# A state-space scan on VectorE and its read-out on GpSimd: the read-out waits one drive longer, and the FFN's inner scaling changes engine

## The chip, the cores and the metric

The kernel runs on one core of a Trainium2 chip. The metric is device time in microseconds of one execution; lower is better. Engines are named TensorE (PE), VectorE (DVE), ScalarE (ACT), GpSimd (POOL) and SyncE (SP, which issues all transfers here).

## The reference, cut to what matters

16 sequences of 256 tokens with 128 channels pass four layers, each with a layer norm in front and a residual addition behind: a linear attention with random features, an FFN whose activations and weights are rounded to FP4 in blocks of 16, a selective state-space mixer (Mamba-like), and the same FFN again.

```python
x = x + attention(layernorm(x))
x = x + ffn(layernorm(x))
x = x + mixer(layernorm(x))
x = x + ffn(layernorm(x))

# mixer, the part that matters here: 256 inner channels, 16 states n
dA = exp(dt[..., None] * A)                     # "decay"
dBu = (dt * u)[..., None] * Bm[:, :, None, :]   # "drive"
h = dA_t * h + dBu_t                            # "scan" over the tokens
y = einsum('lbdn,bln->bld', hs, Cm)             # "read" times C, and a sum over n

# ffn: fp4_quant_dequant of the input of each product
h = silu(fp4_linear(x, w_gate)) * fp4_linear(x, w_up)
return fp4_linear(h, w_down)
```

## The kernel before, in words

The sequences go in eight groups of two (`SEQS`), 512 tokens each. The kernel is a software pipeline of ten turns over these groups. In turn i the group i is `new` (attention), i - 1 is `mid` (attention's end, first FFN `ffn_a`, the mixer up to its drives) and i - 2 is `old` (the mixer's scan and read-out, second FFN `ffn_b`). The order of the work on each engine is written out by hand: every engine has a `body(turn)` with two loops over 16 slots k, and the engines meet by semaphores only (`Events`; `at(group, n)` is the count after n events of that group).

The first loop is called the scan loop here. Slot k handles state k of the old group, in five steps:

- ScalarE: `decay_in`, two exponentials per state (L691), two buffers.
- VectorE: `drive` (L1032), `dtu` times the row of B, both 128x1024 and both in SBUF, result in two PSUM banks.
- VectorE: `scan` (L1043), one `tensor_tensor_scan` over 1024 elements, `decay` from SBUF and the drive from PSUM, result `state` in SBUF, three buffers.
- GpSimd: `read_out` (L566), `state` times the row of C, both in SBUF, result `read`, three buffers.
- TensorE: `sum_states` (L1301), matmuls with the identity that add `read` into two PSUM banks, two slots later.

The rows of B and C (`bc_row`, 512 KB per state, four buffers) are loaded by SyncE; a load waits for the read four states earlier. There is a single PSUM buffer for the drive, so drive k + 1 waits for scan k and scan k + 1 for drive k + 1.

Beside this, each engine's `attention_rest(turn, k)` carries the other work of the slot: statistics of the norms in slots 0, 2 and 15 (`statistics` on VectorE, `deviation` on GpSimd, `normalise` on ScalarE), rounding of the FFN's input in slots 3 and 4, squares and Newton steps of the attention's norms in slots 6 to 10 (GpSimd's Newton steps in slot 9, VectorE's two multiplications L1109 in slot 10), and the FFN's hidden layer for two pairs of tiles: `hidden_start` in slots 7 and 11, `hidden_end` in 8 and 12 (VectorE), then `scale_hidden` in 8 and 12 (GpSimd, L551 and L556: subtract the rounding constant, multiply by the block scale), then `hidden_t` and `down` in 10 and 14 (TensorE) and `ffn_result` in 11 and 14 (VectorE, L1011).

The second loop, called the feature loop here, computes the attention's features, scores and context of the new group (`features` L1017 and L1023, `mask` L1053) and `mixer_rest`: the rest of the mixer for old and mid, and `ffn_b`. Its start needs TensorE's `project` of slot 1, which stands behind `sum_states` of states 14 and 15 in TensorE's order.

Before the change VectorE's slot reads scan k, drive k + 1, other work, and GpSimd's slot reads read k, other work. The last turn has only an old group, and in it the FFN of the group before (`ffn_b_aside`) runs beside the scans, with `scale_hidden` on GpSimd in slots 2 and 6.

Of the kernel before, what the change touches and what calls it, by code (L numbers as in the profile page):

```python
# [19 lines left out]
ALU = mybir.AluOpType  # L20
# [25 lines left out]
SLOTS = SEQS * PAIRS  # L46
# [52 lines left out]
def build(nc, x_in, w_qkv_t, b_qkv, w_out_t, b_out, omega_t, nodes, weights, ln_g, ln_b, in_wx_t,  # L99
# [17 lines left out]
    with ctx:  # L117
# [374 lines left out]
        def _(pool):  # L492
# [68 lines left out]
            def read_out(group, s):  # L561

                pool.wait_ge(state_done.sem, state_done.at(group, s + 1))

                pool.wait_ge(y_ps.sem, y_ps.at(group, max(s + 1 - STATE_BUFFERS, 0)))
                pool.tensor_tensor(  # L566
                    read[:, s % STATE_BUFFERS], state[:, s % STATE_BUFFERS],
                    bc_row[:, s % BC_BUFFERS, 1].unsqueeze(1).broadcast_to([P, DT, TOK]), ALU.mult).then_inc(
                        read_done.sem, 1)

            def attention_rest(turn, k):
# [5 lines left out]
                if turn.has_new and k == 3:  # L577
# [5 lines left out]
                    pool.tensor_tensor(  # L583
                        xab[:], xa[:], bout[:].unsqueeze(1).broadcast_to([P, TILES, C]), ALU.add
                    ).then_inc(residual.sem, 1)
                if turn.has_mid and k in (8, 12):
                    scale_hidden(ffn_a, mid, (k - 8) // 4)
                if turn.is_last and k in (2, 6):
                    scale_hidden(ffn_b_aside, late, (k - 2) // 4)
                if turn.has_new and k == 9:  # L590
# [56 lines left out]

            def body(turn):
                for k in range(SLOTS):
                    if turn.has_old:  # L650
                        read_out(turn.old, k)
                    attention_rest(turn, k)
                for k in range(SLOTS):
                    mixer_rest(turn, k)
                if turn.is_last:
                    scale_hidden(ffn_b, turn.old, 0)
                    scale_hidden(ffn_b_last, turn.old, 1)
# [238 lines left out]
        def _(dve):  # L896
# [107 lines left out]
            def hidden_end(f, group, pair):  # L1004
                round_end(f, group, f.quant_h, f.h[:].rearrange("p t n -> p (t n)"), 8 + 7 * pair
                          ).then_inc(f.h_lifted.sem, 1)

            def ffn_result(f, group, pair, x_src, dst):
                dve.wait_ge(f.down_ps.sem, f.down_ps.at(group, pair + 1))
                tiles = slice(2 * pair, 2 * pair + 2)  # L1010
                dve.tensor_tensor(  # L1011
                    dst[:, tiles], f.out, x_src[:, tiles], ALU.add).then_inc(f.result.sem, 1)
# [60 lines left out]
            def attention_rest(turn, k):  # L1073
# [26 lines left out]
                    hidden_start(ffn_a, mid, (k - 7) // 4)  # L1100
                if turn.has_mid and k in (8, 12):
                    hidden_end(ffn_a, mid, (k - 8) // 4)
                if turn.has_new and k == 10:
                    dve.wait_ge(rnorm_done.sem, rnorm_done.at(new, 1))
                    for b in range(SEQS):
                        rows = slice(CHUNKS * b, CHUNKS * (b + 1))
                        cols = slice(CHUNKS * 2 * HEADS * b, CHUNKS * 2 * HEADS * (b + 1))
                        v = qk[:, rows].rearrange("p t (h d) -> p (t h) d", d=HD)
                        dve.tensor_tensor(  # L1109
                            v, v, rnorm[:, cols].unsqueeze(2).broadcast_to(  # L1110
                                [P, CHUNKS * 2 * HEADS, HD]), ALU.mult).then_inc(zn_done.sem, 1)
# [74 lines left out]
            def body(turn):  # L1186
                for k in range(SLOTS):
                    if turn.has_old:
                        scan(turn.old, k)
                        if k + 1 < SLOTS:  # L1190
                            drive(turn.old, k + 1)
                    if turn.has_mid and k == 0:
                        attention_out(turn.mid, SEQS - 1)
                    attention_rest(turn, k)
                if turn.has_new:
                    features(turn.new, 0)
                for k in range(SLOTS):
# [428 lines left out]
```

## Time and profile before

| | |
|---|---|
| median of 3 runs | 1839.3 us (1839.26 to 1842.27) |
| the profiled execution | 1841.2 us, span of its instructions 1839.4 us |
| VectorE busy | 1398.6 us (76% of the span) |
| TensorE busy, matmuls | 1178.1 us (64%) |
| ScalarE busy | 730.8 us (40%) |
| GpSimd busy | 651.6 us (35%) |
| mean granted clock of TensorE | 0.780 of full speed |
| transfers | 74.74 MB, mean 41 GB/s |

All durations below are of the one profiled execution, in microseconds from the start of its span unless ns is written. Busy time is the time in which an engine executes an instruction; where an instruction is held up after it has started, the holding is inside its duration. The idle time of an engine is put down to what ended it.

### The profile page before, as it was taken

What the parts mean: (1) busy time and instruction counts of PE and PEld (TensorE: products, weight loads), DVE (VectorE), ACT (ScalarE), POOL (GpSimd) and SP (SyncE); (2) the same over time, 40 slices, a digit from 0 to 9 for tenths busy, and PEclk for the clock granted to TensorE, in tenths of its full rate; (3) what the DMA queues carried; (4) which work ended last, traced back from release to release, by engine and by line L of the source; (5) the groups of instructions that cost most, each with busy time, mean ns of one, the idle gap of its engine ahead of it and who ended that gap; (6) DMA issues with size and microseconds to landing.
All of it is one profiled execution on the core that took longest, in us unless ns stands there. A gap on an engine that the chain in (4) does not pass through costs nothing. (4 is left out here: it accounts for less than half of the span.)

```text
span 1839.4 us, 14293 instructions
## 1 busy us (share of the span) xinstructions
PE 1178.1 (64%) x4361; PEld 591.2 (32%) x4361; DVE 1398.6 (76%) x1535; ACT 730.8 (40%) x1293; POOL 651.6 (35%) x484
## 2 busy tenths in 40 slices
PE   4966864786557775587647866477745874444554
PEld 1433332343223432244323432233422442221212
DVE  1744699777996789866997779967898669965964
ACT  2534642554326533264324543255332642243211
POOL 2012244323353144422444233531345223452531
PEclk9967876897768976788778977689767887775765
DMA  2000122010210112001220102101110011202210
GB/s 55 1 6 1 48 75 68 0 48 29 75 46 1 48 58 68 23 1 53 75 68 1 48 29 74 46 1 48 52 68 24 0 54 69 69 0 80 77 33 6
DMA packets 31404, 74.74 MB, mean 41 GB/s; under 512 B 4505, under 2 KB 14562, under 8 KB 31330
## 3 DMA queue, kind: packets, MB, share of 16 engines
q1 hardware_dynamic: 31330, 73.83, 11.7%
q8 instruction: 37, 0.61, 0.1%
q14 instruction: 37, 0.30, 0.1%
HBM read 71.20 MB, written 2.62 MB: 40 GB/s over the span
## 5 line engine op out<-in xcount | busy, mean ns | idle before, releaser
L566 POOL TENSOR_TENSOR read<-state,bc_row 128x1024 f32<-128x1024 f32 x128 | 316.4, 2472 | 453.5 <-DVE state L1043 449.9
L1032 DVE TENSOR_TENSOR bank<-dtu,bc_row 128x1024 f32<-128x1024 f32 x128 | 382.9, 2992 | 34.1 <-POOL dtu L644 20.8
L1301 PE MATMUL bank<-read,ident 128*128 128x512 f32 x512 | 328.5, 783 | 100.7 <-POOL read L566 100.7
L1043 DVE TENSOR_TENSOR_SCAN state<-decay,bank 128x1024 f32<-128x1024 f32 x128 | 291.6, 2278 | 4.7 <-ACT decay L691 0.5
L691 ACT ACTIVATE decay<-dt,neg_a 128x510 f32<-128x510 f32 x256 | 169.3, 711 | 287.6 <-DVE state L1043 286.5
L1301 PEld LDWEIGHTS bank<-read,ident 128*128 128x128 f32 x512 | 120.7, 252 | 246.1 <-issue 123.5
L1053 DVE TENSOR_TENSOR s_sb<-bank,causal 128x512 f32<-128x512 f32 x128 | 87.9, 687 | 134.0 <-PE bank L1251 134.0
L1249 PE MATMUL bank<-feat 64*128 64x256 f32 x512 | 118.1, 487 | 95.2 <-ACT s_sb L702 95.1
L1238 PE MATMUL bank<-znt,omega 128*128 128x512 f32 x256 | 152.0, 678 | 40.2 <-ACT sqf L682 40.2
L679 ACT ACTIVATE expf<-bank,minus_s,root2s 128x512 f32<-128x512 f32 x128 | 99.8, 780 | 119.1 <-PE bank L1238 118.7
L1275 PE MATMUL bank<-s_sb,vext 128*32 128x256 f32 (+1 forms) x1024 | 131.9, 358 | 2.9 <-DVE att L1068 2.4
L702 ACT ACTIVATE s_sb<-bank 128x256 f32<-128x256 f32 x128 | 49.1, 384 | 205.1 <-DVE s_sb L1053 205.1
L1023 DVE SCALAR_TENSOR_TENSOR feat<-expf,scale_f,sqf 128x512 f32<-128x512 f32 x128 | 119.3, 932 | 5.5
L1017 DVE TENSOR_SCALAR expf<-expf 128x512 f32<-128x512 f32 x128 | 87.6, 685 | 37.7 <-ACT expf L679 37.7
L1326 PE MATMUL bank<-ident,a_ffn_h 128*128 128x128 f32 (+1 forms) x102 | 26.2, 430 | 129.6 <-POOL a_ffn_h L556 129.6
L1249 PEld LDWEIGHTS bank<-feat 64*128 64x128 f32 x512 | 51.9, 211 | 166.5 <-issue 151.3
L551 POOL TENSOR_TENSOR b_ffn_rounded<-b_ffn_rounded,b_ffn_magic 128x704 f32<-128x704 f32 x15 | 26.4, 1761 | 187.8 <-DVE b_ffn_rounded L970 187.8
L682 ACT ACTIVATE sqf<-bank 128x512 f32<-128x512 f32 x128 | 76.2, 595 | 0.0
L1238 PEld LDWEIGHTS bank<-znt,omega 128*128 128x128 f32 x256 | 45.2, 205 | 90.3 <-issue 85.6
L1275 PEld LDWEIGHTS bank<-s_sb,vext 128*32 128x32 f32 x1024 | 40.8, 114 | 102.2 <-issue 68.1
L1251 PEld LDWEIGHTS bank<-feat 64*128 64x128 f32 x512 | 68.8, 219 | 7.0
L1251 PE MATMUL bank<-feat 64*128 64x128 f32 x512 | 65.6, 303 | 0.0
(223 smaller groups left out, 1893.3 us busy)
## 6 DMA issues: line engine op xcount, KB each, us to landing
bc_row<-bc_rows SPq DMA_DIRECT2D x128, 512.0 KB, 3.6
xa<-x_dram SPq DMA_DIRECT2D x8, 256.0 KB, 2.7
out_dram<-x SPq DMA_DIRECT2D x8, 256.0 KB, 2.3
omega<-omega_t_dram SPq DMA_DIRECT2D x1, 512.0 KB
bc_rows<-xdbl SPq DMA_DIRECT2D x8, 64.0 KB
wqkv<-w_qkv_t_dram SPq DMA_DIRECT2D x1, 192.0 KB
state<-w_down_dram SPq DMA_DIRECT2D x1, 176.0 KB, 2.5
state<-w_gate_dram SPq DMA_DIRECT2D x1, 128.0 KB, 2.1
```

The costliest lines, as they stand in the source:

```text
L566: pool.tensor_tensor(read[:, s % STATE_BUFFERS], state[:, s % STATE_BUFFERS], bc_row[:, s % BC_BUFFERS, 1].unsqueeze(1).broadcast_to([P, D ...
L679: act.activation(expf[:, s % 2], bank[:, 0], ACT.Exp, bias=minus_s[:], scale=root2s[:]).then_inc(exp_done.sem, 1)
L691: last = act.activation(decay[:, s % 2, k, :, 1:], dt[:, k].rearrange("p (b t) -> p b t", b=SEQS)[:, :, 1:], ACT.Exp, scale=neg_a[:, k, s: ...
L1023: dve.scalar_tensor_tensor(feat[:, s % 2], expf[:, s % 2], scale_f[:], sqf[:, s % 2], ALU.mult, ALU.mult).then_inc(feat_done.sem, 1)
L1032: dve.tensor_tensor(bank[:, DRIVE_BANK:DRIVE_BANK + DT], dtu[:], bc_row[:, s % BC_BUFFERS, 0].unsqueeze(1).broadcast_to([P, DT, TOK]), ALU ...
L1043: dve.tensor_tensor_scan(state[:, s % STATE_BUFFERS].rearrange("p k t -> p (k t)"), decay[:, s % 2].rearrange("p k b t -> p (k b t)"), ban ...
L1053: dve.tensor_tensor(s_sb[:, s % S_BUFFERS].rearrange("p h (k t) -> p h k t", t=P)[:, :, 0:3:2], bank[:, 1:3, 0:SEQ + P].rearrange("p h (k ...
L1238: pe.matmul(bank[:, 0], omega[:, j], znt[:, b], start=True, stop=True).then_inc(proj_ps.sem, 1)
L1249: pe.matmul(bank[:, 1 + h, 0:SEQ], f[:, SEQ:SEQ + P], f[:, 0:SEQ], start=True, stop=True)
L1251: last = pe.matmul(bank[:, 1 + h, SEQ:SEQ + P], f[:, SEQ + P:], f[:, P:SEQ], start=True, stop=True)
L1275: last = pe.matmul(o, columns, scored, start=(k == 0 and below == 0), stop=(k == 1 and below == 1))
L1301: last = pe.matmul(bank[:, 6 + k], ident[:], read[:, s % STATE_BUFFERS, k], start=(s == 0), stop=(s == STATES - 1))
```

## The change

Three things are altered.

1. `read_out` on GpSimd has one more wait: the read of state s waits until drive s + 1 is done (for the last state there is no further drive, and the wait asks for what is long done).
2. VectorE's slot becomes scan k, other work, drive k + 1; GpSimd's slot becomes other work, read k.
3. `scale_hidden` of `ffn_a` leaves GpSimd; VectorE does the same two steps right behind `hidden_end` (`hidden_scaled`). `ffn_b` and `ffn_b_aside` keep theirs on GpSimd.

```diff
@@ -562,6 +562,8 @@  (GpSimd, read_out)
                 pool.wait_ge(state_done.sem, state_done.at(group, s + 1))
 
+                pool.wait_ge(drive_done.sem, drive_done.at(group, min(s + 2, STATES)))
+
                 pool.wait_ge(y_ps.sem, y_ps.at(group, max(s + 1 - STATE_BUFFERS, 0)))
@@ -583,8 +585,6 @@  (GpSimd, attention_rest)
-                if turn.has_mid and k in (8, 12):
-                    scale_hidden(ffn_a, mid, (k - 8) // 4)
                 if turn.is_last and k in (2, 6):
                     scale_hidden(ffn_b_aside, late, (k - 2) // 4)
@@ -647,9 +647,9 @@  (GpSimd, body)
                 for k in range(SLOTS):
+                    attention_rest(turn, k)
                     if turn.has_old:
                         read_out(turn.old, k)
-                    attention_rest(turn, k)
@@ -1005,6 +1005,19 @@  (VectorE)
+            def hidden_scaled(f, group, pair):
+                q = f.quant_h
+                dve.wait_ge(f.h_lifted.sem, f.h_lifted.at(group, pair + 1))
+                dve.tensor_tensor(q.rounded, q.rounded, q.magic, ALU.subtract).then_inc(
+                    f.h_rounded.sem, 1)
+                dve.wait_ge(f.h_rounded.sem, f.h_rounded.at(group, pair + 1))
+
+                dve.wait_ge(f.ht_ps.sem, f.ht_ps.at(group, pair))
+                dve.tensor_tensor(
+                    blocks(f.hq[:].rearrange("p t n -> p (t n)")),
+                    blocks(q.rounded), across(q.scale[:], q.blocks), ALU.mult).then_inc(
+                        f.hq_done.sem, 1)
@@ -1100,6 +1113,7 @@  (VectorE, attention_rest)
                 if turn.has_mid and k in (8, 12):
                     hidden_end(ffn_a, mid, (k - 8) // 4)
+                    hidden_scaled(ffn_a, mid, (k - 8) // 4)
@@ -1187,11 +1201,11 @@  (VectorE, body)
                 for k in range(SLOTS):
                     if turn.has_old:
                         scan(turn.old, k)
-                        if k + 1 < SLOTS:
-                            drive(turn.old, k + 1)
                     if turn.has_mid and k == 0:
                         attention_out(turn.mid, SEQS - 1)
                     attention_rest(turn, k)
+                    if turn.has_old and k + 1 < SLOTS:
+                        drive(turn.old, k + 1)
```

Two places show how the order moves. The first is VectorE around slots 7 to 9 of a middle turn. Before:

```order
L1032 TENSOR_TENSOR bank<-dtu,bc_row 128x1024
L990 SCALAR_TENSOR_TENSOR a_ffn_h<-a_ffn_h,bank 128x704
L995 TENSOR_TENSOR a_ffn_h<-a_ffn_h,bank 128x704
L947 TENSOR_REDUCE a_ffn_qh_scale<-a_ffn_h 128x44
L950 TENSOR_SCALAR a_ffn_qh_scale<-a_ffn_qh_scale 128x44
L953 RECIPROCAL a_ffn_qh_inv<-a_ffn_qh_scale 128x44
L955 TENSOR_TENSOR a_ffn_h<-a_ffn_h,a_ffn_qh_inv 128x704
L1043 SCALAR_TENSOR_TENSOR state<-decay,bank 128x1024
L1032 TENSOR_TENSOR bank<-dtu,bc_row 128x1024
L964 TENSOR_SCALAR a_ffn_magic<-a_ffn_h 128x704
L967 TENSOR_SCALAR a_ffn_magic<-a_ffn_magic 128x704
L970 TENSOR_TENSOR a_ffn_rounded<-a_ffn_h,a_ffn_magic 128x704
```

And of the change, where L1045 is the drive and L1056 the scan (the order names the scan's instruction SCALAR_TENSOR_TENSOR):

```order
L1045 TENSOR_TENSOR bank<-dtu,bc_row 128x1024
L1056 SCALAR_TENSOR_TENSOR state<-decay,bank 128x1024
L964 TENSOR_SCALAR a_ffn_magic<-a_ffn_h 128x704
L967 TENSOR_SCALAR a_ffn_magic<-a_ffn_magic 128x704
L970 TENSOR_TENSOR a_ffn_rounded<-a_ffn_h,a_ffn_magic 128x704
L1011 TENSOR_TENSOR a_ffn_rounded<-a_ffn_rounded,a_ffn_magic 128x704
L1016 TENSOR_TENSOR a_ffn_h<-a_ffn_rounded,a_ffn_qh_scale 128x704
L1045 TENSOR_TENSOR bank<-dtu,bc_row 128x1024
L1056 SCALAR_TENSOR_TENSOR state<-decay,bank 128x1024
```

The slot's other work now stands between scan and next drive, so that a scan follows each drive at once, and two 128x704 steps (L1011, L1016) have been added in slots 8 and 12.

The second place is GpSimd at the end of the scan loop, where the last reads and slot 15's deviation of `norm_b` stand. Before:

```order
L566 TENSOR_TENSOR read<-state,bc_row 128x1024 [waits b_y_in_psum,b_state] x3
L531 TENSOR_SCALAR b_ln_rstd<-b_ln_mv 128x4 [waits b_ln_var]
L533 TENSOR_SCALAR b_ln_rstd<-b_ln_mv 128x4
L535 TENSOR_SCALAR b_ln_shift<-b_ln_mv 128x4
L539 TENSOR_TENSOR b_ln_rstd<-b_ln_rstd,minus_half 128x8 [waits b_ln_eps]
L543 TENSOR_TENSOR b_ln_shift<-b_ln_shift,b_ln_rstd 128x4 [waits b_ln_rstd_ready]
```

And of the change:

```order
L568 TENSOR_TENSOR read<-state,bc_row 128x1024 [waits b_y_in_psum,b_drive,b_state] x6
L531 TENSOR_SCALAR b_ln_rstd<-b_ln_mv 128x4 [waits b_ln_var]
L533 TENSOR_SCALAR b_ln_rstd<-b_ln_mv 128x4
L535 TENSOR_SCALAR b_ln_shift<-b_ln_mv 128x4
L539 TENSOR_TENSOR b_ln_rstd<-b_ln_rstd,minus_half 128x8 [waits b_ln_eps]
L543 TENSOR_TENSOR b_ln_shift<-b_ln_shift,b_ln_rstd 128x4 [waits b_ln_rstd_ready]
L543 TENSOR_TENSOR b_ln_shift<-b_ln_shift,b_ln_rstd 128x4
L568 TENSOR_TENSOR read<-state,bc_row 128x1024 [waits b_y_in_psum,b_drive,b_state]
```

The read of state 15 has moved behind the deviation, and every read has the drive among its waits.

## Rows read from the trace of the kernel before

**Rows 1.** Windows of turn 5: stretch, length, busy times, granted clock, DMA share, GB/s.

```profile
870.40:984.80 114.40, 65.83 (x178) 32.77 (x172) 110.15 (x94) 36.66 (x65) 52.13 (x33) 0.73 0.18 60
984.80:1085.40 100.60, 78.27 (x371) 40.72 (x372) 65.24 (x99) 54.04 (x96) 29.19 (x26) 0.85 0.06 22
```

**Rows 2.** Costliest groups, whole span: busy us, mean ns of one, idle before.

```profile
L1032 DVE TENSOR_TENSOR bank<-dtu,bc_row 128x1024 f32<-128x1024 f32 x128 | 382.9, 2992 | 34.1 <-POOL dtu L644 20.8 <-DVE state L1043 0.9
L566 POOL TENSOR_TENSOR read<-state,bc_row 128x1024 f32<-128x1024 f32 x128 | 316.4, 2472 | 453.5 <-DVE state L1043 449.9 <-PE bank L1301 3.5
L1043 DVE TENSOR_TENSOR_SCAN state<-decay,bank 128x1024 f32<-128x1024 f32 x128 | 291.6, 2278 | 4.7 <-ACT decay L691 0.5
L1109 DVE TENSOR_TENSOR qk<-qk,rnorm 128x512 f32<-128x512 f32 x16 | 23.1, 1485 | 16.6 <-POOL rnorm L602 16.6
...
L955 DVE TENSOR_TENSOR a_ffn_h<-a_ffn_h,a_ffn_qh_inv 128x704 f32<-128x704 f32 x17 | 15.2, 892 | 0.6
```

**Rows 3.** Instructions that touch bc_row: least, median and most ns of one.

```profile
L1032 DVE TENSOR_TENSOR bank<-dtu,bc_row x128: 1223/3410/3424, 224.7 to 1772.5; 128x1024 f32<-128x1024 f32 x128
L566 POOL TENSOR_TENSOR read<-state,bc_row x128: 2340/2351/3334, 228.8 to 1778.4; 128x1024 f32<-128x1024 f32 x128
```

**Rows 4.** VectorE's timeline, two drives in turn 5: start, us, instruction.

```profile
912.11 3.42 DVE L1032 TENSOR_TENSOR bank<-dtu,bc_row 128x1024 f32<-128x1024 f32 x1
...
918.00 3.41 DVE L1032 TENSOR_TENSOR bank<-dtu,bc_row 128x1024 f32<-128x1024 f32 x1
```

**Rows 5.** Timeline of all engines in slots 8 and 9 of turn 5.

```profile
940.30 2.28 DVE L1043 TENSOR_TENSOR_SCAN state<-decay,bank 128x1024 f32<-128x1024 f32 x1
940.46 1.67 POOL L551 TENSOR_TENSOR a_ffn_rounded<-a_ffn_rounded,a_ffn_magic 128x704 f32<-128x704 f32 x1 [3.08 <-DVE a_ffn_rounded L970]
942.21 1.39 POOL L556 TENSOR_TENSOR a_ffn_h<-a_ffn_rounded,a_ffn_qh_scale 128x704 f32<-128x704 f32 x1
...
942.68 2.00 DVE L1032 TENSOR_TENSOR bank<-dtu,bc_row 128x1024 f32<-128x1024 f32 x1
...
947.16 1.23 DVE L1032 TENSOR_TENSOR bank<-dtu,bc_row 128x1024 f32<-128x1024 f32 x1
947.32 1.38 POOL L596 TENSOR_TENSOR newton_t<-newton_t,sumsq_qk 128x128 f32<-128x128 f32 x1
```

**Rows 6.** Timelines of GpSimd, ScalarE and VectorE, slots 2 and 3 of turn 5.

```profile
893.25 0.20 POOL L531 TENSOR_SCALAR a_ffn_ln_rstd<-a_ffn_ln_mv 128x4 f32<-128x4 f32 x1 [3.09 <-DVE a_ffn_ln_mv L940]
...
897.72 2.25 POOL L583 TENSOR_TENSOR xab<-xa,bout 128x512 f32<-128x512 f32 x1
...
895.12 1.65 ACT L667 ACTIVATE a_ffn_xq<-x,a_ffn_ln_shift,a_ffn_ln_rstd 128x128 f32<-128x128 f32 x4 [6.03 <-POOL a_ffn_ln_shift L543]
...
899.47 0.54 DVE L950 TENSOR_SCALAR a_ffn_qx_scale<-a_ffn_qx_scale 128x32 f32<-128x32 f32 x1
```

**Rows 7.** Timelines of GpSimd, TensorE and VectorE where the feature loop begins.

```profile
983.79 2.35 POOL L566 TENSOR_TENSOR read<-state,bc_row 128x1024 f32<-128x1024 f32 x1 [3.69 <-DVE state L1043]
...
989.33 0.36 POOL L543 TENSOR_TENSOR b_ln_shift<-b_ln_shift,b_ln_rstd 128x4 f32<-128x4 f32 x2
...
986.20 1.99 PE L1301 MATMUL bank<-read,ident 128*128 128x512 f32 x4 [1.21 <-POOL read L566]
988.02 1.02 PE L1238 MATMUL bank<-znt,omega 128*128 128x512 f32 x2
...
984.50 0.38 DVE L940 BATCH_NORM_AGGREGATE b_ln_mv<-b_ln_stats 128x2 f32<-128x6 f32 x4
...
989.89 0.43 DVE L1017 TENSOR_SCALAR expf<-expf 128x512 f32<-128x512 f32 x1 [2.68 <-ACT expf L679]
```

**Rows 8.** TensorE's timeline from the second pair's hidden values, turn 5.

```profile
974.27 1.54 PE L1326 MATMUL bank<-ident,a_ffn_h 128*128 128x128 f32 x6 [4.72 <-POOL a_ffn_h L556]
975.61 3.62 PE L1301 MATMUL bank<-read,ident 128*128 128x512 f32 x4
979.02 1.67 PE L1337 MATMUL bank<-wdown,a_ffn_ht 128*128 128x128 f32 x12
```

## The prediction

> **What bounds the kernel now.** I read the windows first, then the costliest groups, the spread of single instructions, and the timeline of one group. The program alternates two loops of 16 slots. In turn 5 the scan loop takes 114.4 us, with VectorE busy for 110.2 of them, so VectorE sets it; the feature loop takes 100.6 us with VectorE busy for 65.2 and no engine full, so chains across engines set it [rows 1]. Eight scan loops run, and seven feature loops lie between them. Most of the predicted gain therefore has to come from VectorE's busy time in the scan loop, and most of the loss from a later start of a feature loop.
>
> In the groups, the drive (L1032) costs 382.9 us in 128 instructions, the scan (L1043) 291.6, GpSimd's read (L566) 316.4 [rows 2]. The reader is to see that drive and scan handle equally many elements, yet the drive's mean is 2992 ns; its spread is 1223/3410/3424 ns (least, median, most), while the read's is 2340/2351/3334 [rows 3]. The two states differ by what GpSimd does: in a slot without other work the drive starts at 912.11 and takes 3.42, and the next starts 5.89 us later [rows 4]. The read is released by the same scan as the drive, so they start together, and 3.41 is the read's 2.35 plus most of a drive of 1.22. The reverse is there too: a drive starts at 947.16 and runs its 1.23, and a small GpSimd multiplication that starts 0.16 after it takes 1.38, ending 0.31 after the drive [rows 5]. The scan, by contrast, at 940.30 keeps its 2.28 while GpSimd works from 940.46 on through the scan; the drive behind it is caught and takes 2.00 [rows 5]. So reads block drives and do not touch scans.
>
> GpSimd's durations carry this argument. The Trainium skill (Perfetto Trace Analysis, GPSIMD spans) warns that they are unreliable and that start-to-start spacing is to be used. The spacing agrees here: a blocked drive is 3.41 - 1.22 = 2.19 longer, as measured on VectorE itself.
>
> **Edit 1: the read waits for the next drive.** The read of slot s then runs beside scan s+1. From the drive's end the read ends at 0.08 + 2.35 = 2.43; the scan ends at about 2.37, and the next drive, released by it, starts at 2.47. They miss each other by a hair. Every drive at 1.22: 382.9 - 128 x 1.22 = 226.7 us saved [rows 2, 3]. What is queued behind the wait is GpSimd's next work and TensorE's sum of that state; TensorE is 58% busy in the loop (65.8 of 114.4 [rows 1]) and reads three buffers deep, so in a steady slot nobody needs the sum. Where VectorE has other work after the scan, the read's last 0.15 us block its first instruction if that has two SBUF inputs: about 4 slots in 7 loops, **+4 us**.
>
> **Edit 2: other work between scan and drive; on GpSimd its share ahead of the read.** This costs nothing by itself, but GpSimd's order makes some reads late. Costs, from the trace:
> - Slot 0, six loops: after the statistics GpSimd's deviation takes 1.85 us, by its twin of slot 2 that begins at 893.25 and releases ScalarE at 895.12 [rows 6], but VectorE's drive goes first (1.22), so it ends 3.0 after the statistics, and the read 0 behind it at 5.4. Drive 2 is due at 3.7 and is held 1.7: **+10 us**.
> - Slots 2 and 3, seven loops: again the deviation ends at 3.0; ScalarE's normalising takes 1.65 [rows 6], so VectorE, there at 3.6, waits to 4.75, about 1.15. Then the read to 5.4 and the residual addition (2.25 in contention [rows 6], half that alone) hold the next small step: today that costs 0.35 (0.54 where 0.19 is usual), I take 1.4. Together 2.2 in six loops and 1.2 in the draining one: **+14 us**.
> - Slot 9: the Newton steps and the multiplications by them lose, over 8 turns, 16.6 idle and 23.1 - 16 x 0.69 = 12.1 blocked [rows 2], 3.6 a turn (0.69 lies on one line with 1.22 for 1024 elements and 0.89 for 704). The new order brings the Newton steps ahead of the read but keeps a read beside the multiplications. Between no gain and 3.6 I take half: **-11 us** in six loops.
> - Slot 15, the largest: read 15 was released by scan 15 at 983.79 and its sum ran at 986.20, then the projection at 988.02 [rows 7]. That projection releases the exponential for which VectorE waited 2.68 [rows 7]. Now the statistics, which end at 984.88, 1.15 after the scan, and the deviation, which took from the read's end at 986.14 to 989.69 [rows 7], stand ahead of read 15: 1.15 + 3.55, and some 0.3 more for the feature steps that block it, 5.0 later. Nothing covers this, since the feature loop starts from that projection: **+34 us** (six times 5.0, and once 4.1 where no feature steps block). Bounds: nothing, if the earlier deviation pays it back, and 6.
> - The last turn keeps its two pairs of hidden scaling on GpSimd, at slots 2 and 6, ahead of the read. The backlog holds one drive by 0.6 and the next by 2.25: **+6 us**.
>
> **Edit 3: the hidden layer on VectorE.** 28 multiplications and subtractions in seven scan loops, 128x704 with two SBUF inputs, 892 ns each by VectorE's step of the same shape [rows 2], 0.92 with the wait between: **+26 us**. GpSimd loses 1.67 + 1.39 a pair [rows 5], which gives nothing directly. In turn 1, bound by its chain, the shorter step gives perhaps **-2 us**. The second half's result is now closer: from the hidden values TensorE's chain is transposes at 974.27, a sum at 975.61 (3.4), down projection 1.67 [rows 8]. The sum waits for read 12, which ends 3.65 after the hidden values; 3.65 + 3.4 + 1.67 = 8.7 against VectorE's 7.3: a wait of 1.5 in seven loops, **+10 us** (bounds 0 and 3).
>
> **Sum.** -226.7 + 4 + 10 + 14 - 11 + 34 + 6 + 26 - 2 + 10 = -136 us. The profiled execution took 1841.2, which gives 1705; the median of the runs is 1839.3, 1.9 lower, so **1704 us**. Per middle turn the scan loop should fall from 114.4 to about 94.5 and the feature loop rise from 100.6 to about 105.5.
>
> **The clock, weighed.** The scan loop had a granted clock of 0.73 [rows 1]; the sum at 975.61 took 3.6 and the one at 986.20 took 1.99 [rows 7, 8], the two levels of 1.2 and 2.4 GHz. I keep the slow sum. The Trainium skill (TensorE: Matmul & The Clock Gate, the HAM clock gate) says that idling lowers the clock and activity restores it; a denser scan loop would by that run faster, which is the first rival.
>
> **Rivals.**
> 1. Denser TensorE work at 2.4 GHz. The same matmuls in 94 us instead of 114 leave shorter gaps. The second-half wait goes (-10), the sum and projection of slot 15 are seldom slow already; if the early deviation also pays back half of the slot 15 delay (-17) and slot 3's wait shrinks (-8), the time is 1704 - 35 = 1669. For it: 0.85 granted in the fuller feature loop [rows 1]. Against: nearly all this work is still released one read at a time. Chance 0.2.
> 2. Chains become the bound. With slots of 3.7 instead of 5.9 us, TensorE's backlog after the projections of slot 3 (at 1.2 GHz a sum of 3.5 fills a slot) can hold ScalarE's tanh and VectorE's slot 7; at 5 us for seven loops, 1740. Against: 65.8 us of TensorE fit into 94. Chance 0.15.
> 3. Slower: the scan pays. It reads its decay from SBUF as the drive reads its operands; if a read beside it blocked it, each of 120 scans would be 2.35 longer where the drive gains 2.19: +19 instead of -227 for the main term, with the other terms +91, so about 1950. It decides from the point where a scan lengthens by (227 - 91) / 120 = 1.1 us. The scan at 940.30 and the spread of all 128 (the group's mean is 2278 [rows 2]) speak against it. Chance 0.03.
> 4. The change does not do what it says: the new wait is already over when the read comes to it, so drives stay at 3.4. Only if GpSimd were always late; it idled 453.5 us before reads [rows 2]. Then about 1839 + 60 = 1900. Chance 0.01.
>
> **How the numbers follow.** The forecast has 0.61, its own range 1685 to 1725 from the bounds above. With rivals 1 and 2 taken in, the range is 1660 to 1745. A measurement here can tell 0.2%, 3.7 us, from no change; only rivals 3 and 4 are above that: faster 0.95, same 0.01, slower 0.04.
>
> **What would show it.** Right: the drive's median near 1.23, the scan's still 2.28, the read's releaser the drive, VectorE's new steps 0.9, read 15 some 5 us after the last scan, a scan loop near 94 and a feature loop near 105. Wrong: scans beyond 3 us; drives with a median over 2; VectorE idle in slots 7 or 11 for TensorE; a feature loop of 100 (then slot 15 cost nothing, and the time is near 1670).

## The result, and the profile after

| | before | after |
|---|---|---|
| median | 1839.52 us (4 runs) | 1705.95 us (4 runs) |
| lowest to highest | 1839.26 to 1842.27 | 1705.04 to 1709.21 |
| ratio | | 0.9274, 95% interval 0.9258 to 0.929 |
| profiled execution, its span | 1841.22, 1839.4 | 1706.21, 1704.1 |
| mean granted clock | 0.780 | 0.811 |
| VectorE busy | 1398.6 (76%) | 1206.6 (71%) |

The change saves 133.6 us; 136 were predicted. In the changed kernel the drive is L1045, the scan L1056, the read L568, the sum over states on TensorE L1315, the down projection L1351.

The costliest groups of the kernel after (busy us, mean ns of one, idle before it and what ended that):

```profile
L1315 PE MATMUL bank<-read,ident 128*128 128x512 f32 x512 | 344.2, 810 | 234.2 <-POOL read L568 234.0
L568 POOL TENSOR_TENSOR read<-state,bc_row 128x1024 f32<-128x1024 f32 x128 | 301.8, 2359 | 328.8 <-DVE bank L1045 249.4 <-issue 75.0 <-PE bank L1315 4.5
L1056 DVE TENSOR_TENSOR_SCAN state<-decay,bank 128x1024 f32<-128x1024 f32 x128 | 292.7, 2287 | 11.9 <-ACT decay L691 0.5
...
L1045 DVE TENSOR_TENSOR bank<-dtu,bc_row 128x1024 f32<-128x1024 f32 x128 | 168.8, 1319 | 25.4 <-POOL dtu L644 20.8 <-DVE state L1056 0.5
...
L1123 DVE TENSOR_TENSOR qk<-qk,rnorm 128x512 f32<-128x512 f32 x16 | 17.0, 1101 | 3.9 <-POOL rnorm L602 3.9
...
L1011 DVE TENSOR_TENSOR a_ffn_rounded<-a_ffn_rounded,a_ffn_magic 128x704 f32<-128x704 f32 x16 | 14.3, 892 | 0.5
L1016 DVE TENSOR_TENSOR a_ffn_h<-a_ffn_rounded,a_ffn_qh_scale 128x704 f32<-128x704 f32 x16 | 14.3, 892 | 0.5
```

Against [rows 2]: the drives fell from 382.9 to 168.8 us, 214.1 less; the scans stayed (2278 ns each before, 2287 now); the read's releaser is the drive; L1011 and L1016 are new on VectorE, 892 ns each.

Instructions that touch bc_row, after (least/median/most ns of one), to be read against [rows 3]:

```profile
L1045 DVE TENSOR_TENSOR bank<-dtu,bc_row x128: 1206/1226/3133, 223.6 to 1645.0; 128x1024 f32<-128x1024 f32 x128
L568 POOL TENSOR_TENSOR read<-state,bc_row x128: 2337/2342/3332, 232.5 to 1648.6; 128x1024 f32<-128x1024 f32 x128
```

The median drive went from 3410 to 1226 ns while the read kept its length: two instructions that had met no longer meet.

Windows of the kernel after: the scan loop and the feature loop of turn 5, and the last turn's scan loop (start:end and length, busy times, granted clock, DMA share, GB/s):

```profile
824.00:917.00 93.00, 64.06 (x177) 30.62 (x174) 87.56 (x99) 36.18 (x65) 43.65 (x28) 0.81 0.22 74
917.00:1023.70 106.70, 80.64 (x373) 41.41 (x373) 63.97 (x97) 53.99 (x96) 30.14 (x26) 0.84 0.06 21
1567.50:1648.50 81.00, 47.19 (x100) 19.78 (x100) 71.19 (x52) 22.73 (x36) 44.72 (x19) 0.71 0.24 81
```

The scan loop of turn 5 fell from 114.4 to 93.0 us, and its feature loop rose from 100.6 to 106.7 [rows 1]. VectorE is now 94% busy in the scan loop (87.56 of 93.00); before it was 96%.

What VectorE waited for (us in total, times, longest), first before, then after:

```profile
DVE x L1011 <- PE bank L1337: 46.9, 15, 8.7
DVE expf L1017 <- ACT expf L679: 37.7, 19, 5.2
```

```profile
DVE expf L1030 <- ACT expf L679: 87.5, 19, 11.1
DVE x L1024 <- PE bank L1351: 62.8, 23, 6.3
```

Here lies what the new order costs: 49.8 us more before the exponentials of the feature loop, 15.9 more before the FFN's result.

The timeline of turn 5 after (start, us, instruction, idle before it): a held drive in slot 0, slots 2 and 3, a steady slot, slot 14, then the end of the scan loop, and two held drives of the last turn.

```profile
832.50 2.35 POOL L568 TENSOR_TENSOR read<-state,bc_row 128x1024 f32<-128x1024 f32 x1
833.36 2.58 DVE L1045 TENSOR_TENSOR bank<-dtu,bc_row 128x1024 f32<-128x1024 f32 x1
...
840.30 1.07 POOL L531 TENSOR_SCALAR a_ffn_ln_rstd<-a_ffn_ln_mv 128x4 f32<-128x4 f32 x1 [1.89 <-DVE a_ffn_ln_mv L940]
...
844.72 0.69 DVE L947 TENSOR_REDUCE a_ffn_qx_scale<-a_ffn_xq 128x32 f32<-128x512 f32 x1 [1.01 <-ACT a_ffn_xq L667]
845.44 1.13 DVE L950 TENSOR_SCALAR a_ffn_qx_scale<-a_ffn_qx_scale 128x32 f32<-128x32 f32 x1
...
857.85 1.23 DVE L1045 TENSOR_TENSOR bank<-dtu,bc_row 128x1024 f32<-128x1024 f32 x1
859.18 2.29 DVE L1056 TENSOR_TENSOR_SCAN state<-decay,bank 128x1024 f32<-128x1024 f32 x1
859.22 2.34 POOL L568 TENSOR_TENSOR read<-state,bc_row 128x1024 f32<-128x1024 f32 x1 [1.37 <-DVE bank L1045]
...
911.83 0.42 DVE L1024 TENSOR_TENSOR x<-bank,x 128x256 f32<-128x256 f32 x1 [1.13 <-PE bank L1351]
...
916.57 0.38 DVE L940 BATCH_NORM_AGGREGATE b_ln_mv<-b_ln_stats 128x2 f32<-128x6 f32 x4
...
920.47 2.34 POOL L568 TENSOR_TENSOR read<-state,bc_row 128x1024 f32<-128x1024 f32 x1
922.86 3.78 PE L1315 MATMUL bank<-read,ident 128*128 128x512 f32 x4 [4.95 <-POOL read L568]
926.43 1.70 PE L1252 MATMUL bank<-znt,omega 128*128 128x512 f32 x2
928.98 0.43 DVE L1030 TENSOR_SCALAR expf<-expf 128x512 f32<-128x512 f32 x1 [10.93 <-ACT expf L679]
...
1588.19 1.59 DVE L1045 TENSOR_TENSOR bank<-dtu,bc_row 128x1024 f32<-128x1024 f32 x1
1592.26 3.13 DVE L1045 TENSOR_TENSOR bank<-dtu,bc_row 128x1024 f32<-128x1024 f32 x1
```

At 857.85 stands the order the prediction wanted: drive, then scan and read side by side, both at full speed. At 917 stands its largest cost: after the statistics end at 916.95, the first exponential step that hangs on the projection behind read 15 (L1030 at 928.98) starts 12.0 us later, where it was 5.0 before (984.88 to 989.89 [rows 7]).

### The profile page after: what moved, and what is told of

It is laid out like the page before. It is cut to its first block and busy times, and to the rows that moved or that the text cites. A ratio compares the mean times of both kernels' runs of the same rounds, so it can differ in the third digit from the quotient of the medians.

```text
span 1704.1 us, 14293 instructions
## 1 busy us (share of the span) xinstructions
PE 1184.0 (69%) x4361; PEld 577.2 (34%) x4361; DVE 1206.6 (71%) x1567; ACT 727.4 (43%) x1293; POOL 594.3 (35%) x452
## 5 line engine op out<-in xcount | busy, mean ns | idle before, releaser
L1315 PE MATMUL bank<-read,ident 128*128 128x512 f32 x512 | 344.2, 810 | 234.2 <-POOL read L568 234.0
L568 POOL TENSOR_TENSOR read<-state,bc_row 128x1024 f32<-128x1024 f32 x128 | 301.8, 2359 | 328.8 <-DVE bank L1045 249.4
L1056 DVE TENSOR_TENSOR_SCAN state<-decay,bank 128x1024 f32<-128x1024 f32 x128 | 292.7, 2287 | 11.9 <-ACT decay L691 0.5
L1315 PEld LDWEIGHTS bank<-read,ident 128*128 128x128 f32 x512 | 114.8, 245 | 393.2 <-POOL read L568 263.5
L1045 DVE TENSOR_TENSOR bank<-dtu,bc_row 128x1024 f32<-128x1024 f32 x128 | 168.8, 1319 | 25.4 <-POOL dtu L644 20.8
L1066 DVE TENSOR_TENSOR s_sb<-bank,causal 128x512 f32<-128x512 f32 x128 | 88.0, 687 | 127.1 <-PE bank L1265 127.1
L1030 DVE TENSOR_SCALAR expf<-expf 128x512 f32<-128x512 f32 x128 | 80.3, 628 | 87.5 <-ACT expf L679 87.5
L640 POOL TENSOR_TENSOR dt<-half_x,tanh_x 128x1024 f32<-128x1024 f32 x8 | 18.7, 2339 | 130.6 <-ACT half_x L854 130.6
```

What stands on the lines that cost most here:

```text
L568: pool.tensor_tensor(read[:, s % STATE_BUFFERS], state[:, s % STATE_BUFFERS], bc_row[:, s % BC_BUFFERS, 1].unsqueeze(1).broadcast_to([P, D ...
L1045: dve.tensor_tensor(bank[:, DRIVE_BANK:DRIVE_BANK + DT], dtu[:], bc_row[:, s % BC_BUFFERS, 0].unsqueeze(1).broadcast_to([P, DT, TOK]), ALU ...
L1056: dve.tensor_tensor_scan(state[:, s % STATE_BUFFERS].rearrange("p k t -> p (k t)"), decay[:, s % 2].rearrange("p k b t -> p (k b t)"), ban ...
L1066: dve.tensor_tensor(s_sb[:, s % S_BUFFERS].rearrange("p h (k t) -> p h k t", t=P)[:, :, 0:3:2], bank[:, 1:3, 0:SEQ + P].rearrange("p h (k ...
L1315: last = pe.matmul(bank[:, 6 + k], ident[:], read[:, s % STATE_BUFFERS, k], start=(s == 0), stop=(s == STATES - 1))
```

## The experiments

Medians are of four runs unless it says otherwise, ratios are against seven runs of the kernel before on the same chip, and changes of a wait or a group are over the whole span. Where the two kernels of a difference ran on different chips, the kernel before varied between them by 2.4 us at most (1839.52 beside the full change, and 1839.76, 1841.90 and 1839.85).

### Do read and drive block each other? Half a read

```diff
 pool.tensor_tensor(
-    read[:, s % STATE_BUFFERS], state[:, s % STATE_BUFFERS],
-    bc_row[:, s % BC_BUFFERS, 1].unsqueeze(1).broadcast_to([P, DT, TOK]), ALU.mult).then_inc(
+    read[:, s % STATE_BUFFERS, 0], state[:, s % STATE_BUFFERS, 0],
+    bc_row[:, s % BC_BUFFERS, 1], ALU.mult).then_inc(
...
-last = pe.matmul(bank[:, 6 + k], ident[:], read[:, s % STATE_BUFFERS, k],
+last = pe.matmul(bank[:, 6 + k], ident[:], read[:, s % STATE_BUFFERS, 0],
```

The kernel before, but the read-out of the second half of the channels is left out: TensorE sums the first half twice.

> The kernel before, with a read of one 128x512 half where there were two; TensorE sums that half twice, so it has the same work, and the second half of the channels is not read out. Theory A (a drive that meets a read waits for exactly the rest of it): the read takes 1.2 us, the drive's median falls from 3.41 to about 2.25 us, the whole to about 1839 - 115 x 1.15 = 1705 us. Rival B (what slows the drive is a fixed price of meeting GpSimd, or lies in the drive's own operands): the drive stays at 3.4 and the time near 1839 us.

One run: 1712.93 us, 8 above what theory A gave; its drive stayed at 2.33, where 2.25 was expected. Instructions that touch bc_row in it:

```profile
L1032 DVE TENSOR_TENSOR bank<-dtu,bc_row x128: 1222/2331/2346, 224.9 to 1648.5; 128x1024 f32<-128x1024 f32 x128
L566 POOL TENSOR_TENSOR read<-state,bc_row x128: 1262/1270/2252, 229.0 to 1653.3; 128x512 f32<-128x512 f32 x128
```

The drive is unchanged in the code, and lost as much as the read beside it: both medians are 1.08 us shorter (3410 to 2331, 2351 to 1270). So the drive waits for the whole of the read, and then runs. It also shows that GpSimd's own durations can be used here; what the prediction called spacing was only the drive's lengthening (2.19, beside a read of 2.35). The Trainium skill (SBUF — State Buffer, Who interferes with whom) says that a VectorE instruction with two SBUF inputs and a GpSimd instruction that reads SBUF exclude each other for a whole instruction, and that one with a single SBUF input is left alone unless it runs in a mode that uses both ports, as copies and tensor_scalar can. These traces agree: 1.08 against 1.08 for the drive, and a scan, whose second input lies in PSUM, keeps its length: 2278 ns on average before the change, 2287 after it, where a read runs beside nearly every one. The next experiment shows the tensor_scalar's side. It also rules out that drive and read only meet over the tile bc_row, which both read: the rounding steps held there share no tile with the read.

### Edit 1 alone: the wait in the old order

```diff
 pool.wait_ge(state_done.sem, state_done.at(group, s + 1))
+pool.wait_ge(drive_done.sem, drive_done.at(group, min(s + 2, STATES)))
```

> The kernel before with edit 1 alone (the read waits for the next drive; order and scaling as before). Theory A (the wait alone frees every drive in slots without other work; in slots with other work the read now stands beside it and blocks the steps with two SBUF inputs or in a fast mode, in slots 3, 4, 6, 8, 10, 12, some 15 us a loop instead of 31, but read 15 stays early): about 1720 us. Rival B (the order is what frees the drives, and with the old order the read only moves from the drive to other work): 1790 us or more.

1706.78 us, ratio 0.9274 (0.9258 to 0.9289): the time of the full change. Its drives as a group, and two small rounding steps from its timeline:

```profile
L1034 DVE TENSOR_TENSOR bank<-dtu,bc_row 128x1024 f32<-128x1024 f32 x128 | 171.3, 1338 | 34.1 <-POOL dtu L646 20.8 <-DVE state L1045 0.9
```

```profile
856.68 2.45 DVE L969 TENSOR_SCALAR a_ffn_magic<-a_ffn_magic 128x512 f32<-128x512 f32 x1
...
882.89 2.54 DVE L969 TENSOR_SCALAR a_ffn_magic<-a_ffn_magic 128x704 f32<-128x704 f32 x1
```

One line brings the whole gain. In the old order drive s+1 is followed by the slot's other work and only then by scan s+1; the read, released by the drive, now meets that work. A rounding step of 0.43 or 0.53 us takes 2.45 or 2.54. Over the span that is 42 us in this group of rounding steps and some 16 in three smaller ones; it is the price that edit 2 removes.

### The full change without edit 1

> The changed kernel without edit 1: order and scaling as after, but the read waits for the scan only. Theory A (the read starts at the scan's end and blocks the other work with two SBUF inputs, or the drive where there is none; some 24 us a loop, to which edit 3 adds 3.7): about 1860 us, no better than the kernel before. Rival B (with other work between scan and drive most reads are over before the drive): 1720 to 1760 us.

1848.05 us, ratio 1.0044 (1.0029 to 1.0059): edits 2 and 3 without the wait are 0.44% slower than the kernel before. Its drives, and two instructions from the timeline of its turn 5:

```profile
L1043 DVE TENSOR_TENSOR bank<-dtu,bc_row 128x1024 f32<-128x1024 f32 x128 | 252.0, 1969 | 25.4 <-POOL dtu L642 20.8 <-DVE state L1054 0.5
```

```profile
903.87 2.45 DVE L965 TENSOR_SCALAR a_ffn_magic<-a_ffn_magic 128x512 f32<-128x512 f32 x1
...
912.12 3.42 DVE L1043 TENSOR_TENSOR bank<-dtu,bc_row 128x1024 f32<-128x1024 f32 x1
```

The group of drives is 130.9 us shorter than before (382.9 to 252.0), and nothing is gained. In slots with other work that work stands behind the scan, and now meets the read in the drive's place: the small steps that are held (two groups of rounding steps, a multiplication and two small scalings) cost some 65 us more. Most of the rest goes to what edits 2 and 3 cost in any case: 28.6 more for the scaling steps less 12.7 of waits for the Newton steps, and 47.3 more of waiting for the exponentials behind the late read 15 (85.0 against 37.7), of which 7.3 come back in steps held less. Reading the drive group alone would have promised 131 us.

### Edit 3 alone, in the kernel before

```diff
-                if turn.has_mid and k in (8, 12):
-                    scale_hidden(ffn_a, mid, (k - 8) // 4)
...
                     hidden_end(ffn_a, mid, (k - 8) // 4)
+                    hidden_scaled(ffn_a, mid, (k - 8) // 4)
```

> The kernel before with edit 3 alone (ffn_a's hidden scaling on VectorE). Theory A (VectorE bounds the scan loop, and GpSimd, no longer busy at that time, starts reads 8 and 12 and their neighbours together with the drives: three drives a loop that took 2.00, 1.23 and 2.00 us go to 3.4; some 3 us come back at the Newton steps): 3.7 + 5 - 3 = 5.7 us a loop, 7 loops: about 1880 us. Rival B (VectorE's added work alone): 1865 us. Rival C (VectorE does it faster than GpSimd, and that helps): under 1839 us.

1890.2 us, ratio 1.0262 (1.0247 to 1.0277), 48 us slower. Its drives:

```profile
L1043 DVE TENSOR_TENSOR bank<-dtu,bc_row 128x1024 f32<-128x1024 f32 x128 | 416.2, 3252 | 32.5 <-POOL dtu L642 19.7 <-DVE state L1054 0.5
```

The scaling steps cost their 28.6 us, and the drives 33.3 more: GpSimd is no longer busy with the scaling when the scan ends, so its read starts in time to block the drives that it had missed. Against this stand 25.5 us at the Newton steps and the multiplications by them (39.7 to 14.2). The exponentials also wait 15.3 more (53.0 against 37.7), which was not foreseen. The start of the feature loop in turn 5 shows why:

```profile
1013.37 3.78 PE L1313 MATMUL bank<-read,ident 128*128 128x512 f32 x4 [4.04 <-POOL read L566]
...
1019.55 0.43 DVE L1028 TENSOR_SCALAR expf<-expf 128x512 f32<-128x512 f32 x1 [5.16 <-ACT expf L677]
```

Read 15 is not late here, but TensorE was idle for 4.04 us before its sum, and the sum took 3.78 instead of 1.99 [rows 7]. The exponential waits 5.16 instead of 2.68, and so in each of six loops: 2.5 us a loop for the slower matmuls alone.

### Edits 1 and 3 in the old order

> The kernel before with edits 1 and 3, its order kept. Against the wait alone (1706.8 us) VectorE has 3.7 us a loop more and gets back two drives of 2.00 (0.8 each), most of 1.6 us idle before the multiplications of slot 10, and perhaps the wait in slot 14. Theory A: about 1705 to 1712 us, so edit 3 is worth nothing by itself here. Rival B (VectorE's work counts in full): 1733 us.

1711.07 us, ratio 0.9293 (0.9277 to 0.9308). Beside the wait alone, edit 3 costs 4 us (1706.78 to 1711.07), but the two intervals overlap (0.9258 to 0.9289 there), so it is not shown that it costs anything in this order. Two groups of it, the rounding steps and the drives, and the rounding steps' group of the kernel after:

```profile
L967 DVE TENSOR_SCALAR a_ffn_magic<-a_ffn_magic 128x704 f32<-128x704 f32 (+1 forms) x25 | 54.8, 2193 | 0.9
...
L1045 DVE TENSOR_TENSOR bank<-dtu,bc_row 128x1024 f32<-128x1024 f32 x128 | 160.6, 1255 | 32.5 <-POOL dtu L644 19.6 <-DVE state L1056 0.5
```

```profile
L967 DVE TENSOR_SCALAR a_ffn_magic<-a_ffn_magic 128x704 f32<-128x704 f32 (+1 forms) x25 | 12.4, 496 | 0.9
```

This kernel differs from the full change by edit 2 alone, so the pair is edit 2's ledger beside the other two; edit 2 by itself was not run. It saves 42.4 us of rounding steps (54.8 to 12.4) and loses on the waits for the exponential (38.7 to 87.5, +48.8), for the down projection (44.8 to 62.8, +18.0) and on the drives (160.6 to 168.8, +8.2); smaller items, the Newton steps' 13.8 foremost, go the other way, and the balance is 5 us in favour, again with overlapping intervals.

### The full change without edit 3

```diff
+                if turn.has_mid and k in (8, 12):
+                    scale_hidden(ffn_a, mid, (k - 8) // 4)
...
-                    hidden_scaled(ffn_a, mid, (k - 8) // 4)
```

> The changed kernel with edit 3 undone: ffn_a's hidden scaling is on GpSimd again, in slots 8 and 12, ahead of that slot's read. Theory A (GpSimd's backlog makes the reads late and they catch two drives each time, as in the last turn, where the two drives took 1.59 and 3.13 us, and the later hidden values keep VectorE waiting in slot 11 or 14): 3.7 us a loop saved on VectorE, 4.5 lost in drives, 3 to 5 in waits, 7 loops: about 1740 us. Rival B (the 26 us on VectorE were a plain loss): about 1680 us.

1729.14 us, ratio 0.9399 (0.9385 to 0.9413): edit 3 saves 23 us inside the new order, where rival B expected it to cost. Theory A had the right sign but put too much weight on the drives. The drives, and what VectorE waits for:

```profile
L1047 DVE TENSOR_TENSOR bank<-dtu,bc_row 128x1024 f32<-128x1024 f32 x128 | 174.5, 1363 | 23.9 <-POOL dtu L646 19.7
```

```profile
DVE x L1026 <- PE bank L1352: 91.7, 23, 8.7
...
DVE qk L1124 <- POOL rnorm L604: 19.1, 8, 5.1
```

The drives are only 5.7 us above the full change's 168.8. The loss is in waits: 28.9 us more for the down projection (91.7 against 62.8), since the hidden values come late from GpSimd, and 15.2 more for the Newton steps behind them (19.1 against 3.9). Against this stand the 28.6 us of scaling steps that VectorE doesn't have to do. So edit 3 shortens a chain from VectorE through GpSimd to TensorE and back; it does not mainly clear the drives. The same run is edits 1 and 2 without the third, and it is 22 us slower than the wait alone (1706.78): edit 2 pays only where edit 3 is made too.

### The full change, read 15 ahead of the deviation

```diff
                 for k in range(SLOTS):
+                    if turn.has_old and k in (SLOTS - 1,):
+                        read_out(turn.old, k)
                     attention_rest(turn, k)
-                    if turn.has_old:
+                    if turn.has_old and k not in (SLOTS - 1,):
                         read_out(turn.old, k)
```

> The changed kernel, but in slot 15 GpSimd does read 15 before the deviation, as before the change. Theory A (the late read 15 delays the whole feature loop and nothing pays it back): the feature loop of turn 5 falls from 106.7 to about 100.6 us, six such turns and one of some 4 us, so 1706 - 41 = about 1665 us. Rival B (the earlier deviation pays for it): 1695 to 1706 us, since norm_b's chain is then later by as much.

1667.95 us, ratio 0.9062 (0.9049 to 0.9076), 38.0 below the full change. VectorE's wait for the exponential, and the start of turn 5's feature loop:

```profile
DVE expf L1032 <- ACT expf L681: 35.7, 19, 5.2
```

```profile
899.38 1.98 PE L1317 MATMUL bank<-read,ident 128*128 128x512 f32 x4 [0.34 <-POOL read L568]
...
903.08 0.43 DVE L1032 TENSOR_SCALAR expf<-expf 128x512 f32<-128x512 f32 x1 [2.67 <-ACT expf L681]
```

The wait is back at its old size (35.7, and 37.7 before the change). And the sum behind read 15 takes 1.98 us after 0.34 idle, where it took 3.78 after 4.95 idle in the full change: TensorE's granted clock was 0.50 of full speed (1.2 GHz) during those 3.78 us, after 1.00 in the sum before the idle stretch (915.92), and 1.00 (2.4 GHz) during the 1.98 here. The late read thus costs more than its delay.

### Read 0 first as well

The same edit with `k in (0, SLOTS - 1)`.

> The changed kernel with GpSimd's read ahead of the deviation in slots 0 and 15. Theory A (in slot 0 too the deviation makes the read late, and drive 2, which took 2.58 us, gives back 1.35; norm_a's chain is 2.4 later but TensorE and ScalarE wait for nothing there that VectorE needs soon): 1668 - 6 x 1.35 = 1660 us. Rival B (norm_a's later chain holds back the projections and what stands behind them on TensorE): 1668 to 1680 us.

1650.8 us, ratio 0.896 (0.8947 to 0.8974), 17 below the kernel with read 15 first. The scan loop of turn 5 in that kernel and in this one, and a drive of this one in slot 0:

```profile
804.10:897.90 93.80, 64.42 (x174) 30.48 (x171) 87.28 (x97) 36.20 (x65) 44.57 (x29) 0.78 0.21 73
```

```profile
798.30:889.90 91.60, 61.38 (x175) 28.36 (x172) 86.14 (x99) 36.20 (x65) 44.91 (x29) 0.85 0.23 75
```

```profile
807.60 1.23 DVE L1047 TENSOR_TENSOR bank<-dtu,bc_row 128x1024 f32<-128x1024 f32 x1
```

The drive that took 2.58 in the full change takes 1.23, and all drives together fell from 168.8 to 160.7, the 8.1 us expected. That leaves 9. VectorE waits less for TensorE (59.3 against 65.4 for the down projection, 130.2 against 133.9 for L1068), TensorE is busy 16.3 us less for the same matmuls (1170.9 to 1154.6), and the granted clock of this scan loop is 0.85 instead of 0.78. That fits matmuls run at 2.4 GHz more of the time, but no run set the clock apart from the order, so it stays open.

### Read 2 first too

The same edit with `k in (0, 2, SLOTS - 1)`.

> As the kernel with the read first in slots 0 and 15 (1650.8 us), and in slot 2 too. Theory A (which order is right depends on who waits: in slot 2 VectorE itself waits for the norm that hangs on the deviation, so its wait of 1.0 us grows by 2.4 and only the 0.95 of a held small step comes back): +1.5 us in seven loops, about 1661 us. Rival B (a read that starts at once is always better): 1644 us or less.

1662.56 us, ratio 0.9039 (0.9023 to 0.9054), 12 worse than the kernel before it. VectorE's wait for ScalarE's normalised input, here:

```profile
DVE a_ffn_qx_scale L949 <- ACT a_ffn_xq L669: 29.7, 8, 3.7
```

and with reads 0 and 15 first:

```profile
DVE a_ffn_qx_scale L949 <- ACT a_ffn_xq L669: 10.7, 8, 3.6
```

19.0 us more, of which 12 are in the time; 5.8 come back in the small step behind it (L952, 7.2 to 1.4), which GpSimd's residual addition no longer holds. So the change is right to put slot 2's deviation first: there VectorE waits for what the deviation releases, while TensorE, the only one to use read 2, is busy with projections until after it is done (with reads 0 and 15 first, the read ends at 818.2 in turn 5 and its sum follows other matmuls at 821.42 without idle time). At slots 0 and 15 it is the other way about.

### Everything in the scan loops on VectorE

```diff
                 if turn.is_last and k in (2, 6):
-                    scale_hidden(ffn_b_aside, late, (k - 2) // 4)
+                    pass
...
                     hidden_end(ffn_b_aside, late, (k - 2) // 4)
+                    hidden_scaled(ffn_b_aside, late, (k - 2) // 4)
```

On top of reads 0 and 15 first.

> The changed kernel with the read ahead of the deviation in slots 0 and 15, and the last turn's hidden scaling (slots 2 and 6) on VectorE as well. Theory A (what cost 1.59 + 3.13 us in two drives, each of two times, was GpSimd's backlog): every drive near 1.23 us but the one at the Newton steps; 2 x 2.3 us back in drives and some 2 in slot 5's wait, against 3.7 more on VectorE: 1651 - 3 = about 1648 us. Rival B (VectorE's added steps count in full, the backlog's drives were hidden by waits anyway): 1654 us.

1643.94 us, ratio 0.8936 (0.8921 to 0.8951), 7 less, with intervals that just meet. Its drives:

```profile
L1047 DVE TENSOR_TENSOR bank<-dtu,bc_row x128: 1205/1225/1453, 223.0 to 1578.5; 128x1024 f32<-128x1024 f32 x128
```

The longest of 128 drives takes 1453 ns, beside a Newton step on GpSimd: none is held by a read any more. But the drives gave back only 2.6 us (160.7 to 158.1), not the 4.6 of the expectation, which took the pair of 1.59 and 3.13 to occur twice; the last turn has one 3.13. More came from VectorE's wait for the FFN's result in that turn, 6.07 before this edit and 1.44 with it. This is the fastest kernel of the study, 62 us below the full change.

## Why the prediction was right

The time (1705.95 against 1704) and the sign came out, and so did the mechanism: the half read shows that the read's length is what the drive lost, and edit 1 alone gives the whole gain. The sum was close because its errors cancel, which is luck. One step failed: the term for slot 15 took the late matmuls to keep their speed, put 5.0 us on a loop with 6 as the upper bound, and the loops lost 7.1. Its terms, each against what the profile after shows:

| term | predicted, us | measured, us |
|---|---|---|
| drives, with slot 0 and the last turn | -226.7 + 10 + 6 = -210.7 | -214.1 |
| new steps on VectorE | +26 | 28 x 0.892 = +25.0 |
| slots 2 and 3 | +14 | +10.7 |
| Newton steps and the multiplications, six loops | -11 | -13.7 |
| second half's wait for the down projection, seven loops | +10 | +14.2 |
| slot 15, read 15 late | +30 + 4 = +34 | +42.5 + 5.4 = +47.9 |
| tail of the read on other work | +4 | +1.2 |
| turn 1 | -2 | -2.3 |

The measured column adds to -131.1; the spans differ by 135.3 (1839.4 to 1704.1). The rest is waits that had no term: L1066's for TensorE fell from 134.0 to 127.1, and in the last turn the FFN's result (4.9) and L990 (1.9) wait longer, L1144 (3.3) and L1174 (1.1) shorter.

**Drives.** Slot 0 held one drive in each of six loops to 2.58, 1.35 over: 8.1 us where 10 stood. The last turn held three drives, by 0.37, 1.91 and 0.37, 2.6 us where 6 stood: the backlog of the second hidden scaling held one drive and not two. Six more drives, one a loop beside a Newton step, took 1.44 or 1.45 instead of 1.22, 1.3 us in all that no term held.

**Slots 2 and 3.** Idle 1.01 and a small step of 1.13 instead of 0.54, 1.6 a loop, where 2.2 stood. Over the span the wait before L947 grew by 7.1 (3.6 to 10.7) and the small step L950 by 3.6 (3.6 to 7.2), 10.7 together.

**Newton steps.** The 39.7 us of idle and busy time in [rows 2] (23.1 + 16.6) are now 17.0 + 3.9. Spread evenly over 8 turns the 16.6 were misread: 3.9 of them lie in turn 0 and stay, 5.1 in turn 1 (they are in its row), and 7.6 in the six loops. There the idle time is gone altogether, and of the held time half (6.1), since a read still lies beside the first multiplication: 13.7 in all, where I had taken half of a larger possible gain.

**Second half.** Of the 15.9 us that this wait grew by, 14.2 lie in slot 14 of seven loops, where the sum of a read runs ahead of the down projection: 1.1 to 2.7 each, 2.0 on average, where I took 1.5 with bounds of 0 and 3. The rest is the last turn, 4.9 longer, and turn 1, 3.2 shorter (8.73 to 5.52).

**Turn 1.** Its FFN's result comes at 153.70 instead of 156.08, 2.3 us earlier against the start of its FFN, for all the four new steps: the shorter chain pays them back, close to the 2 I gave it.

**Slot 15.** This is the mis-sized term. The wait for ScalarE grew by 49.8; the exponentials' multiplications were blocked less (L1017's 87.6 us are L1030's 80.3), so the net is 42.5, or 7.1 in each of six loops. The seventh feature loop shows its cost elsewhere, in the wait before L1174 (8.72 instead of 3.32, 5.4 more where 4.1 stood). Read 15 started 4.7 us after scan 15 (scan 15 ended at 915.78) instead of 0.08, 4.6 later where I had 5.0. But I priced only the delay, by the old sum of 1.99 us [rows 7]. TensorE had nothing to do for 4.95 us before that sum, and ran it in 3.78 at a granted clock of 0.50, which is 1.2 GHz: some 1.8 us a loop that the delay itself brought, and the projection behind it took 1.70 instead of 1.02 [rows 7]. Delay, sum and projection make 4.6 + 1.8 + 0.7 = 7.1; the exponential in turn 5 starts 12.0 instead of 5.0 after the statistics, 7.0 later. The step that failed is "1.15 + 3.55, and some 0.3 more", which moved a matmul in time and left its speed as it was. Edit 3 alone shows that part without the delay: 2.5 us a loop. That most of this term is avoidable the run with read 15 first shows: 38.0 us back.

**The tail of the read.** It is there, but small. The first step behind a scan in slots 8 and 12 is L964, and it takes 564 ns at the median where it took 514 before, in the rounding of the FFN's input 462 where it took 412:

```profile
L964 DVE TENSOR_SCALAR a_ffn_magic<-a_ffn_h x17: 518/564/662, 127.0 to 1690.2; 128x704 uint32<-128x704 uint32 x17
```

The two groups grew by 0.9 and 0.4 us, 1.2 of it in the scan loops. I had counted on 0.15 us in first steps with two SBUF inputs; the ones held are steps with one.

**The loops.** Forecast 94.5 and 105.5, measured 93.0 and 106.7: the scan loop gained more and the feature loop paid more, for the reasons above.

**Rivals.** The first, denser TensorE work at a higher clock, was partly there: the scan loop's granted clock rose from 0.73 to 0.81, but the wait for the down projection grew. The read of slot 15 had to be moved before the kernel came near its 1669. The second fell: VectorE stays busy for 94% of the scan loop, and L990 of the first FFN, the step of slots 7 and 11, waits in turn 1 only. The third fell: scans take 2287 ns. The fourth fell: the reads wait for the drive, and without that wait the kernel takes 1848.

**What the prediction missed** lies beside its sum: it priced edits 2 and 3 as costs that come with edit 1, without asking what each brings. Together they bring nothing that can be measured: the wait alone takes 1706.78, all three 1705.95. Edit 2 removes 2.45 us rounding steps and pays with a late read 15, and without edit 3 it costs 22 us; edit 3 brings nothing measurable in the old order and saves 23 in the new.

The range of 1685 to 1725 was also narrower than the bounds it was said to come from: those of slot 15, the Newton steps and the second half, all taken low or all high, add up to about 1649 and 1734.

## What to carry to other kernels

Where a GpSimd instruction and a VectorE instruction with two SBUF inputs are released by the same event, let the GpSimd one wait for the VectorE one if the next on VectorE reads only one operand from SBUF (here one wait gave 7.3%), and then go slot by slot through what stands between them: whatever follows on VectorE in the read's 2.35 us must be of the kind that isn't blocked, and ahead of a read may only stand what somebody waits for more. And don't judge such an edit by the group that it shortens: without the wait the drives fell by 131 us and the kernel got no faster (1848.05 against 1839.76 on the same chip).

## What the runs showed of the hardware that was not expected

- A small instruction is blocked like a long one. A VectorE TENSOR_SCALAR of 128x704, 0.53 us alone, took 2.54 beside a read, although it has one SBUF input, a kind that the prediction left out of its rule for the read's tail (it did count one such step, L950, as held); the scan of 128x1024, with one SBUF and one PSUM input, never did. A GpSimd step of 128x4, 0.20 us in [rows 6], took 1.07 when it started at 840.30 beside a drive that ran from 840.13 to 841.34.
- Blocking costs as long as the other instruction has left, not a share of the speed: shortening the read by 1.08 us shortened the drive beside it by 1.08.
- The same four matmuls took 3.78 us after 4.95 us of idle time and 1.98 after 0.34, at granted clocks of 0.50 and 1.00, the two levels of 1.2 and 2.4 GHz. A late start therefore cost its 4.6 us and 1.8 more, and where the start was on time but 4.04 us of idle time lay before it (edit 3 alone), the 3.78 came all the same.
